# A decoder layer in float16 pairs on one core: row maxima of the first cross-attention batch from natural scores instead of turned ones

## What is computed

```python
def reference(x, ctx_2048, mask_BxS2_fk1, ...):
    x = _layernorm(x + _L0_attn_ref(x, ...))                      # self-attention, 16 heads
    x = _layernorm(x + _L0_xattn_ref(ctx_2048, x, mask, mask, ...))
    x = _layernorm(x + _L0_ffn_ref(x, w1, b1, w2, b2))            # 512 -> 2048 -> 512
    return x

def _L0_xattn_ref(src, tgt, src_mask, tgt_mask, ...):             # 8 batches, 8 heads of 64
    k, v, q = ...                                                 # projections, masked
    scores = jnp.einsum('bthd,bshd->bhts', q, k) / np.sqrt(HEAD_DIM)
    scores = jnp.where(src_mask[:, None, None, :] == 0, -jnp.inf, scores)
    attn = jax.nn.softmax(scores, axis=-1)
    tgt_update = jnp.einsum('bhts,bshd->bthd', attn, v)
    return jnp.einsum('btf,of->bto', concatenate([tgt, tgt_update]), W_out) + b_out
```

## Time and profile before

| | |
|---|---|
| median of 3 runs | 1925.07 us (1924.38 to 1926.57) |
| the profiled execution's own time | 1928.58 us |
| its span | 1926.8 us |
| PE busy | 1799.6 us (93%) |
| DVE busy | 1377.1 us (71%) |
| ACT busy | 768.2 us (40%) |
| mean granted TensorE clock | 0.973 |
| second half begins | about 820 us |
| heads of the first batch | 858 to 954 us |

### The profile page before, as it was taken

The page is one execution under the profiler, slowest core; times in us unless marked ns, Lnnn a source line. Parts: engine busy times, 40 slices in busy tenths (PEclk is TensorE's granted clock), DMA queues, the critical chain, the costliest instruction groups (busy, mean ns, idle before and its releaser), DMA issues. The chain is left out here.

```text
span 1926.8 us, 32971 instructions
## 1 busy us (share of the span) xinstructions
PE 1799.6 (93%) x12476; PEld 994.1 (52%) x12476; DVE 1377.1 (71%) x1421; ACT 768.2 (40%) x1208; POOL 559.3 (29%) x576
## 2 busy tenths in 40 slices
PE   7999999999999989866689999999999999999988
PEld 3565465546554646444445545455454554555543
DVE  2899998999899999556547567566665775757621
ACT  3323222222222222234527456274472653736522
POOL 3135965695468335400100201102003020020010
PEclk9999999999999999977899999999999999999999
DMA  8436356525643566564151620715307135061000
GB/s 207 127 78 151 80 142 151 118 74 147 155 93 98 129 170 142 148 152 150 29 104 28 115 68 7 137 39 86 96 1 134 48 63 119 2 127 33 12 34 22
DMA packets 322654, 183.97 MB, mean 95 GB/s; under 512 B 225584, under 2 KB 278832, under 8 KB 322511
## 3 DMA queue, kind: packets, MB, share of 16 engines
q1 hardware_dynamic: 316448, 178.37, 40.3%
q10 hardware_dynamic: 6062, 3.49, 0.8%
HBM read 94.75 MB, written 33.55 MB: 67 GB/s over the span
## 5 line engine op out<-in xcount | busy, mean ns | idle before, releaser
L1175 POOL TENSOR_TENSOR q<-q,x_hi 128x512 f16<-128x512 f32 x28 | 41.0, 1494 | 642.8 <-ACT x_hi L1473 642.8
L1203 PE MATMUL b_ff<-x2T_hi,w1T_hi 128*128 128x512 f16 x512 | 195.3, 381 | 2.3 <-DVE x2T_lo L1549 2.3
L1203 PE MATMUL b_ff<-x2T_lo,w1T_hi 128*128 128x512 f16 x512 | 195.1, 381 | 0.0
L1203 PE MATMUL b_ff<-x2T_hi,w1T_lo 128*128 128x512 f16 x512 | 195.0, 381 | 0.0
L1598 DVE SCALAR_TENSOR_TENSOR top<-b_st,mleast,top 128x512 f16<-128x512 f32 x192 | 144.1, 751 | 59.5 <-PE b_st L1230 40.0
L1549 DVE TENSOR_TENSOR p_lo<-k,p_hi 128x1024 f16<-128x1024 f32 x128 | 162.2, 1267 | 30.8 <-ACT p_hi L1420 30.8
L1452 ACT ACTIVATE k<-b_st,mbias 128x512 f32<-128x512 f32 x256 | 161.5, 693 | 42.2 <-PE b_st L1251 42.2
L785 DVE TENSOR_TENSOR prod<-q,k 128x4096 f32<-128x4096 f32 x32 | 142.2, 4445 | 17.7 <-ACT q L661 16.9
L578 PE MATMUL sm_b<-cT_hi,wsT_hi 128*128 128x256 f16 x512 | 141.1, 276 | 13.7 <-DMA cT_lo<-rows_lo 12.4
L544 PE MATMUL pj_b<-winT_hi,xT_hi 128*128 128x512 f16 x384 | 146.8, 382 | 1.1 <-DVE winT_lo L852 1.1
L544 PE MATMUL pj_b<-winT_lo,xT_hi 128*128 128x512 f16 x384 | 146.5, 382 | 0.0
(11 more groups left out here) (269 smaller groups left out, 4385.4 us busy)
## 6 DMA issues: line engine op xcount, KB each, us to landing
cn<-in_ctx_dram SPq DMA_DIRECT2D x64, 256.0 KB, 3.1
k<-kT_scratch SPq DMA_DIRECT2D x24, 512.0 KB, 7.6
x<-in_x_dram SPq DMA_DIRECT2D x32, 256.0 KB, 3.2
x_scratch<-x SPq DMA_DIRECT2D x32, 256.0 KB, 2.1
q<-x_scratch SPq DMA_DIRECT2D x8, 1024.0 KB, 5.6
q<-x_scratch SPq DMA_DIRECT2D x32, 256.0 KB, 3.3
out_dram<-q SPq DMA_DIRECT2D x32, 256.0 KB, 4.6
xn<-in_x_dram SPq DMA_DIRECT2D x24, 256.0 KB, 2.9
```

Source lines behind the costliest of these rows:

```text
L1203: mm = pe.matmul(out, a, c, start=(start and n == 0), stop=end)
```

## The change

Only the heads of the first batch are rewritten; the loop over the other seven batches issues the same instructions in the same order, with semaphore counts shifted by 8. For the first batch:

- The maxima come from natural scores, queries on the partitions and the 512 keys along the row (`natural_scores`), made in the banks `st_b[2]` and `st_b[3]` in turn, up to one head ahead. DVE takes the maximum along the row in one operation, with the mask added as a float32 row (`natural_tops`, tensor_tensor_reduce), and negates the four columns. Each tensor_tensor_reduce is two instructions in the program, one over 128x512 and one that reads out a 128x1 result, both of the kind ISA. `turned_tops` and `negated_maxima` fall away.
- The turned scores of a head are made afresh in `st_b[0]` and `st_b[1]` in turn, both products together (`both_scores`), each once the exponential two before it is done.
- The weight blocks move: number 0 ahead of the heads, 2h+1 in the middle of head h and 2h+2 at its end, where before 0 and 1 came ahead and the pairs 2h+2, 2h+3 in heads 0 to 6.
- The fourth quarter of the queries is split by ACT and DVE before the first weight block and not after it, and one 128x512 tensor_scalar makes the mask row `mneg`.

```diff
+            def natural_scores(h, half):
+                for tt in (2 * half, 2 * half + 1):
+                    if h or tt >= 2:
+                        pe.wait_ge(s["topped"], 4 * h + tt - 1)
+                    pe.matmul(st_b[2 + tt % 2][:, :], q1[:, h, tt * P:(tt + 1) * P], k1[:, h, :], start=True,
+                              stop=True).then_inc(s["first_filled"], 1)
+
+            def both_scores(h, half):
+                for st in (2 * half, 2 * half + 1):
+                    if st == 0:
+                        pe.wait_ge(s["mr_copied"], h + 1)
+                    if h or st >= 2:
+                        pe.wait_ge(s["st_exp"], 4 * h + st - 1)
+                    keys = slice(st * P, (st + 1) * P)
+                    pe.matmul(st_b[st % 2][:, :], k1[:, h, keys], q1[:, h, :], start=True, stop=False)
+                    pe.matmul(st_b[st % 2][:, :], k2[:, h, keys], q2[:, h, :], start=False,
+                              stop=True).then_inc(s["st_filled"], 1)
...
+            def first_heads():
+                weight_transposes(0)
+                pe.wait_ge(s["q_masked"], 4)
+                maximum_row(0, 0)
+                for h in range(H2):
...
+                    if h + 1 < H2:
+                        natural_scores(h + 1, 0)
+                    both_scores(h, 0)
+                    if h == 1:
+                        pe.wait_ge(s["v_ld"], 80)
+                    if h:
+                        values(0, h - 1)
+                    if h + 1 < H2:
+                        natural_scores(h + 1, 1)
+                    weight_transposes(2 * h + 1)
+                    both_scores(h, 1)
+                    if h + 1 < H2:
+                        maximum_row(0, h + 1)
+                        weight_transposes(2 * h + 2)
+                output_x1(None)
+                values(0, H2 - 1)
...
+            def natural_tops(h, half):
+                for tt in (2 * half, 2 * half + 1):
+                    dve.wait_ge(s["first_filled"], 4 * h + tt + 1)
+                    if h or tt:
+                        dve.wait_ge(s["topped"], 4 * h + tt)
+                    dve.tensor_tensor_reduce(top[:, :], st_b[2 + tt % 2][:, :], mneg, 1.0, NEG, ALU.add, ALU.max,
+                                             mx[:, h % 2, tt:tt + 1]).then_inc(s["topped"], 1)
+                if half:
+                    dve.wait_ge(s["topped"], 4 * h + 4)
+                    dve.tensor_scalar(mz[:, 4 * (h % 2):4 * (h % 2) + 4, D2], mx[:, h % 2, :], -1.0, None,
+                                      ALU.mult).then_inc(s["negm"], 1)
```

More of the change, by code:

```diff
@@ L1001, in phase_b @@
     raw, b2_n = [oT[i][0:(2, P)[i], 0:2, :].rearrange("p a b -> p (a b)").bitcast(F32) for i in range(2)]
-    f16o = [sb(f"f16o{i}", [P, E], F16) for i in range(2)]
+    f16o_both = sb("f16o", [P, 2, E], F16)
+    f16o = [f16o_both[:, i, :] for i in range(2)]
+    mneg = f16o_both[:, :, :].rearrange("p a b -> p (a b)").bitcast(F32)
+    mx = sb("mxb", [P, 2, 4], F32)
     x1_hi = [sb(f"x1_hi{i}", [P, E], F16) for i in range(4)]
@@ L1370, in output_rest, with first_queries_and_scores @@
                              (w.ones[:, 0:P], rows_b[:, :]), s["om_filled"], start=False)
+            def first_queries_and_scores():
+                for i in range(3):
+                    queries(0, i, first=True)
+                queries(0, 3, slice(None, 8))
+                pe.wait_ge(s["k_ld"], 48)
+                pe.wait_ge(qs_ld[0][0], 48)
+                natural_scores(0, 0)
+                queries(0, 3, slice(8, None))
+                natural_scores(0, 1)
             def queries_and_first_scores(b, ff):
                 for i in range(3):
-                    queries(b, i, first=ff is None)
-                if ff is not None:
-                    x2_transposes(ff)
+                    queries(b, i)
+                x2_transposes(ff)
                 queries(b, 3, slice(None, 8))
-                if ff is not None:
-                    pe.wait_ge(s["x2t_lo"], 4 * ff + 2)
+                pe.wait_ge(s["x2t_lo"], 4 * ff + 2)
                 pe.wait_ge(s["q_masked"], 4 * b + 2)
@@ L1445, in relu, with exponentials @@
                                saturate=False).then_inc(s["relu"], 1)
-            def exponentials(b, h, half):
+            def exponentials(b, h, half, banks=4):
                 for st in (2 * half, 2 * half + 1):
@@ L1517, in _ @@
             first_x1_high()
-            for i in range(3):
+            for i in range(4):
                 queries_hi(0, i)
@@ L1521, in _ @@
             act.wait_ge(s["rows_made"], 4)
-            heads(0, None)
+            first_heads()
             def batch(b, rows):
```

114 lines of the change are left out of this document (74 added, 40 removed).

## The result

The changed kernel takes 1884.42 us, median of four runs (1882.00 to 1884.78), against 1925.82 for the kernel before on the same chip: a ratio of 0.9778 [0.9759, 0.9797]. The sign was right, the size was not.

What follows compares the result with a forecast made beforehand. It took a chain through PE, DVE and ACT, none of them full, to set the pace; start, head 0, heads 1 to 6, head 7 and low clock summed to 28.5 us saved, from 1925.07 to 1896.6 us, range 1887 to 1903.

Steps and rivals of the forecast that it cites:

- the start: First batch, from first scores at 848.06 us through four tops: both scores of head 0 were to start at 855.0 us.
- heads 1 to 6 at full clock: First batch: six heads at 8.5 us each, 51 us, from 864.8 to 915.8 us.
- I let a quarter of heads 1 to 6 run at 1.2 GHz: Clock term: pace 9.15 us a head instead of 8.5, six heads 3.9 us more, heads 0 and 7 about 0.4.
- two score banks would then be worse than four: Argument for the rival that PE becomes the bound (0.16): fewer PSUM banks in turn keep the clock oscillating; 1904 to 1916 us.
- The price of a natural top: DVE's row maximum with its read-out in the first batch's heads: 0.9 to 1.1 us, taken as 1.0 each.
- the half-rate rival: Rival, chance 0.10: a natural top runs at half rate, 1.53 us each, 10.6 us a head; 14 us saved, 1911 us.
- DVE for one head, now the longest queue: Steady head of the first batch: DVE work of 8.1 us plus about 0.4 idle sets 8.5 us per head.
- Head 0, 9.8 us: First head, with waits for weight block 2 until 863.9 us: 9.8 us instead of 16.68, head 1 beginning at 864.8.
- Head 7, 6.0 us: Last head of the first batch: last weight block, values, transposes, two exponentials and two waits, 6.0 us to the output projection.
- PE at 6.0 us: PE's work per head at 2.4 GHz: 6.0 us, under DVE's 8.5, so the four added matmuls cost nothing.
- I take no loss there: From output projection to next queries: the chain moves with the heads' end, the loop's instructions are the same, 0 us lost.
- the rivals: PE the bound (0.16), tops at half rate (0.10), slower (0.04), gain given back behind the heads (0.04), no effect (0.03).

Runs made afterwards that it cites:

- e1: The changed kernel with each of its 32 natural tops done twice on VectorE; 10.63 us a head, ratio 0.9850.
- e5: The changed kernel with ScalarE's copy of the maximum row moved behind the second rounding of the probabilities; 7.71 us a head, ratio 0.9750.
- e3: The changed kernel with TensorE's dropped wait for all 32 exponentials restored ahead of the first batch's output projection; 1885.87 us, ratio 0.9782.
- e2: The changed kernel with each of its 32 natural score matmuls issued twice, the second alone signalling; 8.39 us a head, ratio 0.9786.
- e6: The changed kernel with batch 1's eight x1 transposes issued ahead of its value loads on SyncE; batch 1 122.49 us, ratio 0.9751.
- e11: The kernel before with batch 1's eight x1 transposes issued ahead of its value loads on SyncE; batch 1 122.84 us, ratio 0.9963.
- e13: The kernel before with 24 long-satisfied waits (12 instructions) added between TensorE's first batch and its loop; 1923.44 us, ratio 0.9971.
- e15: The changed kernel with the moves of e5 and e6, and loads of weight blocks 2 and 3 ahead of the last query copies; 1872.89 us, ratio 0.9702.
- e9: The kernel before with 50 long-satisfied waits added between TensorE's first batch and its loop; 1923.63 us, ratio 0.9974.
- e14: The changed kernel with 104 long-satisfied waits (52 instructions) added ahead of TensorE's loop; 1888.82 us, ratio 0.9793.

## Why the prediction was wrong

In the profiled executions I forecast 1900.1 us and got 1884.78, 15.3 apart. Half of it lies ahead of the output projection, which I put at 926.1 and which started at 918.44. By steps of my sum, the time at the low clock was too large by 4.3 us, the start by 1.7, head 7 by 1.15 and heads 1 to 6 at full clock by 0.7, and head 0 too small by 0.2:

- **"I let a quarter of heads 1 to 6 run at 1.2 GHz", 3.9 us, and 0.4 at the ends.** The largest miss. Heads 1 to 6 took 50.32 us, less than my 51 at full clock. The low clock was confined to heads 0 to 2, next to the waits for block 2 (2.54 and 1.17 us; a clock of 0.61 from 860 to 864 us) and for block 4 (1.57 us; 0.68 from 872 to 876 us); heads 3 to 6 have 0.99 or 1.00 in every kernel with natural tops. TensorE's share, 6.76 of 8.17 us, is higher than my 6.0 of 8.5. The Trainium skill ("TensorE: Matmul & The Clock Gate", "A second HAM failure mode: psum-queue depth-cycling") tells of a kernel that cycled through PSUM banks with small idles and whose clock went up and down. That two score banks would then be worse than four was my own inference, and it is not borne out: two banks in turn ran at 1.00 in steady heads. What raised the clock, no run separates from the rest of the change.
- **The price of a natural top, 1.0 us.** It is 0.83 from start to start, under my range of 0.9 to 1.1 and even under the 0.88 of a top before, though a read-out of 0.08 was added to it. Float32 from PSUM and float32 from SBUF together did not halve the rate, 687 ns for 512 elements, which answers the half-rate rival. The Trainium skill's rule beside it ("Vector Engine (DVE) Microarchitecture Reference", "Points that are easy to get wrong") is on two SBUF sources, where a natural top has one in PSUM, so it says nothing for or against that rule. With the first part's 0.85 us it makes both scores start at 853.30 for my 855.0.
- **"DVE for one head, now the longest queue", 8.5 us.** Nearly the right number (8.17) for a wrong reason, which is luck. VectorE's queue is 7.2 us by the trace, and the cycle that I summed, with the row, its copy and the second p_hi, is 7.7 by e1. The pace is the loop over the one buffer of rounded probabilities, which I had in no sum; e5 shows it. Had I charged tops at 0.83, my sum would have said 7.4 + 0.4 = 7.8, close to that cycle and too low for the head. The 0.4 of idle time in it was also added up wrongly: 0.4, 0.5 and 1.0 are 1.9 and not 2.2, which leaves 0.2.
- **Head 0, 9.8 us:** 9.97, right, with the wait for block 2 where I put it.
- **Head 7, 6.0 us:** 4.85. I missed that a wait is dropped there; e3 prices it at 1.7 us of the projection's start (head 7 is 6.52 there, over my 6.0) and at nothing of the whole.
- **PE at 6.0 us:** 6.76, covered as I said (e2: 0.22 us for 0.87 added).

The other half is **"I take no loss there", behind the heads**, which also took no gain. It was 7.7 us: 2.5 in batch 1, mostly the scatter of one wait and the clock around it (e6, e11); 3.8 in batches 2 to 7 (4.2 at the loop's returns), which e13 gives to the place of the loop; and 1.4 in the last stretch. That last one is scatter too: it is 74.6 in e3 and 73.5 in e15, whose code there is the same. The sentence that the chain of batch 1 "starts from the heads' end and moves with it" was wrong in that the transposes moved 37.9 us earlier (974.66 to 936.76) and TensorE's arrival only 36.

Of the rivals none came. My aside that no instruction of the kind ISA ran on VectorE before is wrong by the compiled program, which had six, though its trace shows no custom reduction on VectorE. My reading of the earlier trace rows was off by one slice: the three low ones are 819 to 963 us and not 870 to 1010. And my base was one execution: the kernel before has heads 1 to 6 at 76.4 us in it, at 79.0 to 80.5 in the four others with the same heads, so part of the gain in the whole was there to be had by any kernel that keeps the clock.

## What to carry to other kernels

Busy sums name a candidate for the bound, not the bound. To find it, follow the single-buffered tiles round once (who writes, who reads last, who may write again) and add that turn up before believing the fullest engine. A forecast from one profile of a stretch whose clock falls should carry the scatter of that clock, and a stretch without edits can still move by some us: look at what waits there for a transfer, and at the idle time at a loop's return. A queue's idle gap is the place for loads that are needed first.

## What the runs showed that I had not expected

- TensorE's first matmul after its loop returns stands idle by up to 2.5 us with no releaser. Twelve idle instructions ahead of the loop took the sum over six returns from 8.5 to 2.9 us; 25 (e9), 64 (e14) and 76 (e2) gave 4.5, 4.7 and 5.2.
- The same wait can cost twice: 4.06 us for a transpose, and a low clock after it. The 8 us from the start of batch 1, the wait among them, have a mean clock of 0.66, and the next 8 have 0.92; without the wait (e11) batch 1 is 6.4 us shorter, in that one execution. Where TensorE arrived later and waited 0.66 us (e3), the clock stayed at 1.00.
